# A fused attention and feed-forward kernel: keys' transposes moved from TensorE to VectorE and DRAM, first keys first, packed keys ahead of packed queries

## The reference

```python
x = L0_attn_x                                  # (16, 1024, 256)
xn = _layernorm(x, axis=-1)
x = x + attn(xn, Wqkv, Wout) + ffn(xn, W1, b1, W2, b2)

# attn: 16 heads of 16, segments of 512 rows; a segment's keys are every 8th row of it (64 keys)
scores = einsum('bhspd,bhskd->bhspk', q4, k4)             # q scaled by 16 ** -0.5
c = max(scores, over each block of 64 query rows)         # per key column
w = exp(scores - c)
out = einsum('bhsnmk,bhskd->bhsnmd', w, v4) / (sum(w, -1) + 1e-10)
return out @ Wout.T
# ffn
return relu(xn @ W1 + b1) @ W2 + b2                       # hidden width 1024
```

## Time and profile before

| | us |
|---|---|
| median of 3 runs | 1060.14 |
| lowest and highest | 1059.68, 1060.82 |
| the profiled execution, its device time | 1064.19 |
| its span from first to last instruction | 1062.2 |
| granted TensorE clock | 1.0 of full speed all through |

### The profile page before, as it was taken

How to read it: one execution, slowest core, us unless ns; L and a number is a source line. 1 busy time by engine, 2 the same in 40 slices (tenths; PEclk the granted TensorE clock), 3 DMA queues, 4 the chain that set the end, 5 groups by cost and what they waited for, 6 DMA issues and landing times.

```text
span 1062.2 us, 19202 instructions
## 1 busy us (share of the span) xinstructions
PE 1042.0 (98%) x5397; PEld 809.4 (76%) x5397; DVE 837.7 (79%) x1464; ACT 648.1 (61%) x1081; POOL 623.2 (59%) x489
## 2 busy tenths in 40 slices
PE   5999999999999999999999999999999999999998
PEld 4677777777787777787777777777877777877777
DVE  7987888878877887888878888788888878887752
ACT  5656665666666566666666656666565665656663
POOL 6355665656556556555656656565665565556564
PEclk9999999999999999999999999999999999999999
DMA  5157877687877778777778776868777787767754
GB/s 193 35 151 217 222 212 210 180 230 205 240 211 200 207 204 230 219 216 204 205 216 226 221 199 183 236 197 244 211 196 206 204 231 212 212 176 217 196 145 148
DMA packets 151895, 214.14 MB, mean 202 GB/s; under 512 B 27072, under 2 KB 95808, under 8 KB 151872
## 3 DMA queue, kind: packets, MB, share of 16 engines
q1 hardware_dynamic: 151728, 213.73, 72.4%
q10 hardware_dynamic: 144, 0.13, 0.0%
HBM read 100.01 MB, written 58.20 MB: 149 GB/s over the span
## 4 chain that ended last, share of the span: by engine, by line
PE 87%; DVE 5%; DMA 4%; issue 2%; SPq 1%; ACT 1%; DVEq 0%; ACTq 0%
PE h_bank L1081 38%; PE y_bank L1081 37%; PE s_banks L1156 5%; PE misc L1260 3%; PE s_banks L1260 2%; PE misc L1081 2%; DVE xn L858 1%; DMA k_pack<-k_dram 1%; DVE s_max L875 1%; DMA w_exp<-w 1%; DMA xt_dram<-z 1%; DVE w_exp L881 1%; DMA xt_raw<-xt_dram 1%; SPq L371 1%; DVE q_lo L924 0%
## 5 line engine op out<-in xcount | busy, mean ns | idle before, releaser
L534 POOL TENSOR_TENSOR h_lo<-h_full,h_hi 128x512 fp32r<-128x512 f32 x256 | 337.6, 1320 | 378.9 <-ACT h_full L625 376.9
L631 ACT ACTIVATE w_exp<-w_exp 128x512 f32<-128x512 f32 x256 | 161.6, 633 | 247.8 <-DVE w_exp L881 245.9
L623 ACT ACTIVATE h_hi<-h_bank,b_cols 128x512 fp32r<-128x512 f32 x256 | 174.7, 682 | 68.2 <-PE h_bank L1081 61.7
L1081 PE MATMUL h_bank<-xt_hi,w_hi 128*128 128x512 f32 x512 | 206.6, 403 | 0.0
L1081 PE MATMUL h_bank<-xt_lo,w_hi 128*128 128x512 f32 x512 | 200.3, 391 | 0.0
L1081 PE MATMUL h_bank<-xt_hi,w_lo 128*128 128x512 f32 x512 | 199.6, 390 | 0.0
L1081 PE MATMUL y_bank<-h_hi,w_hi 128*128 128x512 f32 x496 | 193.5, 390 | 0.2 <-ACT w_exp L631 0.2
L1081 PE MATMUL y_bank<-h_hi,w_lo 128*128 128x512 f32 x496 | 193.1, 389 | 0.0
L1081 PE MATMUL y_bank<-h_lo,w_hi 128*128 128x512 f32 x496 | 193.1, 389 | 0.0
L875 DVE TENSOR_REDUCE s_max<-s_banks 128x8 f32<-128x512 f32 x252 | 169.3, 672 | 29.0 <-PE s_banks L1156 28.5
L881 DVE TENSOR_TENSOR w_exp<-s_banks,s_max 128x512 f32<-128x512 f32 x252 | 174.2, 691 | 10.9
(11 more groups left out here) (146 smaller groups left out, 1542.6 us busy)
## 6 DMA issues: line engine op xcount, KB each, us to landing
q_pack<-q_hi SPq DMA_DIRECT2D x240, 128.0 KB, 2.5
rden_rows<-rden_dram SPq DMA_DIRECT2D x128, 128.0 KB, 4.6
x_b<-x SPq DMA_DIRECT2D x32, 512.0 KB, 4.7
x_raw<-x SPq DMA_DIRECT2D x31, 512.0 KB, 4.9
yt_dram<-y_mem SPq DMA_DIRECT2D x124, 128.0 KB, 3.5
y_mem<-yt_dram SPq DMA_DIRECT2D x31, 512.0 KB, 4.5
out<-x_b SPq DMA_DIRECT2D x31, 512.0 KB, 3.1
q_pack<-q_lo SPq DMA_DIRECT2D x120, 128.0 KB, 2.4
```

The costliest lines, as they stand in the source:

```text
L534: pool.tensor_tensor(h_part[1][:, i % HBUF], h_full[:, i % HBUF], f32(h_part[0][:, i % HBUF]), ALU.subtract).then_inc(h_lo, 1)
L623: act.activation(h_part[0][:, i % HBUF], h_bank[i % 2][:], ACT.Relu, bias=b1_cols[:, i:i + 1]).then_inc(h_hi, 1)
L631: act.activation(w_exp[:, pair], w_exp[:, pair], ACT.Exp).then_inc(w_ready, 1)
L1081: mm = pe.matmul(ps, stationary[a], moving[b], start=start and c == 0 and n == 0, stop=stop and c == len(pairs) - 1 and n == 2, skip_group ...
```

## The change

1. **Keys' blocks.** From step 2 on, PE no longer transposes the keys. At the end of an odd step, between the residual add and the transposes of y, DVE normalises the keys of the next even step and transposes their 32x32 blocks into a part of `z` (`transpose_key_blocks`). SP writes them to `xk_dram` in four DMAs (`key_blocks_to_dram`, after `pack(s, 1)`) and reads them back turned, into `xn_keys` (`keys_in`, after `den_spread`). ACT's `keys_hi` waits for that read, and `keys_hi` and `keys_lo` read SBUF in place of PSUM. For this POOL's `inverse_deviation` stands ahead of the tail's two `hidden_lo` in place of behind them. The large `transpose_blocks` of the even step, which writes the same `z`, waits for the keys' writes.
2. **Packed keys** are issued ahead of `pack(s, 0)`, and wait for all scores of the step, which read the old ones. The read of y is split in two halves, and where a step packs keys, the second half waits for the keys' writes to DRAM.
3. **The first step.** The first keys have statistics and `rstd` of their own ahead of the rows' ones. x of segment 1 is loaded behind two weights, and its statistics are taken later. ACT copies the first queries ahead of a half of w2. POOL clears `q_pack` in the lead step in place of the start. (Keys of segments 0 and 1, and of step 0, are still transposed by PE.)
4. **One residual add**, that of step 1, stands behind POOL's tile 4 in place of tile 2.

```diff
@@ SP
-                load_x(1, 1)
                 sp.dma_start(wkv_raw, ...)
                 sp.dma_start(wq_raw, ...)
+                load_x(1, 1)
...
             def pack_keys(s):
-                sp.wait_ge(k_out, (s + 1) * 32)
+                sp.wait_ge(s_psum, (s + 2) * PAIRS)
...
+            def key_blocks_to_dram(s):
+                sp.wait_ge(z_keys_ready, s + 1)
+                for i in range(P // PW):
+                    sp.dma_start(xk_dram[:, :, i].rearrange("j c n -> c j n"),
+                                 z_keys[PW * i:PW * (i + 1)]).then_inc(xk_out, 16)
+            def keys_in(s):
+                sp.wait_ge(xk_out, (s + 1) * 32)
+                sp.dma_start(xn_keys[:].rearrange("p (a k) -> p a k", a=DH),
+                             xk_dram.rearrange("(a j) c i n -> (j c) a (i n)", a=DH)).then_inc(xk_in, 16)
...
-            def y_from_dram(s):
+            def y_from_dram(s, keys):
                 sp.wait_ge(y_out, (s + 1) * 64)
-                sp.dma_start(y_mem[:, 1], ...).then_inc(y_in, 16)
+                for half, blocks in enumerate((slice(0, 2), slice(2, 4))):
+                    if half == 1 and keys:
+                        sp.wait_ge(k_out, (s + 2) * 32)
+                    sp.dma_start(y_back[:, blocks]..., yt_dram[:, :, blocks]...).then_inc(y_in, 16)
...
                 if norm:
+                    pack_keys(s)
                     pack(s, 0)
-                    pack_keys(s)
                     pack(s, 1)
+                if load and par == 1:
+                    key_blocks_to_dram(s)
                 if attention:
                     den_to_dram(s + 1)
                 if norm:
                     pack(s, 2)
                 if attention:
                     den_spread(s + 1)
+                if load and par == 1:
+                    keys_in(s)
@@ POOL
-                    if i == 2 and ffn:
+                    if i == (4 if isinstance(s, int) and s == 1 else 2) and ffn:
                         residual(s - 1, 1 - par)
...
+                if load:
+                    inverse_deviation(s + 3, 1 - par)
                 segment, tail = tail_tiles(s, attention)
                 for i in tail:
                     hidden_lo(segment, i)
-                if load:
-                    inverse_deviation(s + 3, 1 - par)
@@ ACT
             def keys_hi(s):
-                act.wait_ge(xkey_psum, s + 4)
+                if by_tensor(s):                      # s <= 0
+                    act.wait_ge(xkey_psum, s + 4)
+                else:
+                    act.wait_ge(xk_in, s * 8)
...
-                weight_hi(w2_half(w2_raw, 0), ...)
                 queries_hi(-2, 0)
+                weight_hi(w2_half(w2_raw, 0), ...)
@@ DVE, step
-                    if n == 0 and keys:
-                        normalise_keys(s + 2)
...
                 elif ffn:
+                    if load and par == 1:
+                        normalise_keys(s + 3)
+                        transpose_key_blocks(s + 3)
                     output_blocks(s)
@@ PE, step
-                    if i == KEY_TILES[0] and norm and par == 0:
-                        transpose_keys(s)
```

More of the change, by code:

```diff
@@ L246, in score_bank, with keys_transposed @@
             return s_bank[n % 2]
+        def keys_transposed(s):
+            return key_banks(s)[0][:, 0:DH * P] if by_tensor(s) else xn_keys[:]
         def transpose_banks(s):
@@ L277, in iterations, with tiles @@
                 fixed(s)
-        def tiles(par):
-            return T + 1 - par
+        def tiles(s, par):
+            return T if isinstance(s, int) and s == 0 else T + 1 - par
         def tile_steps(s, ffn):
@@ L447, in opening_step @@
                 keys_to_dram(0)
+                sp.wait_ge(k_out, 32)
+                pack_keys(0)
                 pack(0, 0)
-                pack_keys(0)
                 pack(0, 1)
@@ L583, in step, with first_keys_deviation @@
                     hidden_lo(segment, i)
-                if load:
-                    inverse_deviation(s + 3, 1 - par)
+            def first_keys_deviation():
+                pool.wait_ge(first_keys_stats, 1)
+                pool.wait_ge(consts_made, 3)
+                pool.tensor_tensor(var_eps[:, T:T + 1], mean_var[:, T:T + 1, 1], eps[:, T:T + 1],
+                                   ALU.add).then_inc(first_keys_var, 1)
+                pool.wait_ge(first_keys_var, 1)
+                pool.tensor_tensor(rstd[:, T:T + 1], var_eps[:, T:T + 1], minus_half[:, T:T + 1],
+                                   ALU.pow).then_inc(first_keys_rstd, 1)
+                pool.wait_ge(first_keys_rstd, 1)
             def first_step():
+                first_keys_deviation()
                 inverse_deviation(0, 0)
@@ L811, in mean_variance @@
             def mean_variance(s, par):
-                for t in range(tiles(par)):
+                for t in range(tiles(s, par)):
                     op = dve.bn_aggr(mean_var[:, t], stats_of(s)[:, t])
@@ L823, in normalise_keys, with keys_normalised @@
                 dve.wait_ge(rstd_ready, s + 1)
-                dve.wait_ge(xkey_psum, past(s))
+                if isinstance(s, int) and s <= 2:
+                    dve.wait_ge(xkey_psum, s)
+                else:
+                    dve.wait_ge(xkey_hi, s)
+                    dve.wait_ge(xkey_lo, s)
+                keys_normalised()
+            def keys_normalised():
                 dve.tensor_scalar(xn_keys[:], x_keys[:], mean_var[:, T, 0:1], rstd[:, T:T + 1],
@@ L862, in normalise, with transpose_key_blocks, transpose_blocks @@
                 op.then_inc(xn_ready, 1)
-            def transpose_blocks(s):
+            def transpose_key_blocks(s):
+                dve.wait_ge(xn_keys_ready, s + 2)
+                dve.transpose(z_keys, xn_keys[:].rearrange("p (j n) -> p j n", n=PW)).then_inc(z_keys_ready, 2)
+            def transpose_blocks(s, keys):
+                if keys:
+                    dve.wait_ge(xk_out, s * 32)
                 dve.wait_ge(xn_ready, s + 3)
@@ L1042, in first_step @@
                 drain_kv(-2)
+                statistics(1, 1)
                 statistics_done(1)
```

41 lines of the change are left out of this document (27 added, 14 removed).

## The result

| | before | after |
|---|---|---|
| median, us | 1060.68 (6 runs) | 1068.35 (6 runs) |
| lowest and highest | 1059.68, 1061.94 | 1065.67, 1069.67 |
| ratio, with its 95% interval | | 1.0069 (1.0057 to 1.008) |
| span of the profiled execution | 1062.2 | 1063.8 |

The kernel became 0.7% slower; the forecast was 1061.7 in a range of 1052 to 1073. The profile of after is of the fastest of its six executions, so a second one was taken later (1071.44, span 1069.6; the median of that series is 1067.32 beside 1061.37 for before, ratio 1.0049, 1.0031 to 1.0067). The second profile is of the slowest execution of its series. Both are read here. A stand is a stretch in which PE does nothing.

The account below looks back on a forecast made before the run. PE, busy 98% of the span, was taken as the bound. Terms -3.1 + 5.9 - 1.5 + 3.0 - 1.0 - 1.1 - 0.6 = +1.6 gave 1061.7 from 1060.14; own range 1056 to 1068, all cases 1052 to 1073.

Parts of the forecast that it names:

- Taken off PE: Two key transposes between products of y and h go, 0.22 in each of 14 even steps: -3.1 us.
- The keys' chain: Keys through DVE and DRAM reach PE's keys' projection late, 0.4 a step: +5.9 us (0 to +11).
- rstd is there at 485.1: Step 14, POOL: moved var_eps and rstd follow the statistics, taking 0.27 and 1.18.
- Late reads of y: Where y lands late, the keys behind the residual add come later too: +3 us (0 to 7.4).
- Packed keys first: PE's stands of 2.4 for packed keys go with their earlier issue: -1.5 us (0 to -2.4).
- Step 28: A third to two thirds of PE's 1.40 stand are left, as DVE is 1.3 ahead: -1.0 us.
- Step 1: Later residual add shortens DVE's xn; PE's 0.66 before queries and 0.3 before a score go: -1.1 us.
- The front: First step: ACT's copy of the queries ahead of w2 frees DVE before the first scores: -0.6 us (0 to -0.7).
- Rival (a): Keys arrive in time at the projection; +5.9 and most of +3 go: about 1054, chance 0.25.
- Rival (b): POOL's h_lo locks out DVE's denominators' guard; transpose_k stands 0.9 each even step: +12.6, about 1074, chance 0.12.
- Rival (c): Y's second half comes 0.5 behind DVE's need in every odd step: +7, about 1069, chance 0.13.

Follow-up runs that it names:

- experiment 10: Changed kernel with DVE normalising the keys and transposing their blocks ahead of the residual add, not behind it: 1072.77, ratio 1.0105 to before.
- experiment 11: Kernel of experiment 10 with the keys' read also issued ahead of the denominators' reads in SP's queue: 1071.98, ratio 1.0097 to before.
- experiment 7: Changed kernel with POOL's first tail h_lo waiting for the keys' normalisation, but packed queries first and y in one read again: 1058.05, ratio 0.9962 to before.
- experiment 8: Kernel before with only packed keys first and y read in halves: 1061.2 beside 1061.37, ratio 0.9994.
- experiment 2: Changed kernel without packed keys first, halves of y and later residual add; keys' new way and front stay: 1070.82, ratio 1.0093 to before.
- Experiment 1: Changed kernel with the keys' new way undone and inverse_deviation back behind POOL's tail, all else kept: 1059.2 beside 1060.63, ratio 0.9991.
- experiment 3: Changed kernel with the keys' read issued ahead of the denominators' two reads in SP's queue: 1059.68, ratio 0.9993 to before.
- experiment 5: Changed kernel with the keys' read issued later, behind the fourth packed queries in SP's queue: 1115.02, one execution.

## Why the prediction was right, and where it was off

The range held and the time came out on the slower side, as the sum had it, but with +7.3 and +5.2 us in the two series (by the ratios) in place of +1.6. The two medians lie at the edge of the forecast's own range (1056 to 1068); the rest of 1052 to 1073 is there for the rivals. By its own terms:

- **Taken off PE, -3.1:** right. The rows at 490.55 to 491.01 show it.
- **The keys' chain, +5.9:** the mechanism was right link by link (locked keys 1.22 to 1.39, issue 6.45 behind the blocks, read 2.27 to 2.47 where 2.4 was taken), its size was not. The stand is 0.4 to 1.2, 0.77 on average, where the sum had 0.3. Counted back from PE's need and averaged over the 14 steps of the first profile, the keys are normalised 0.25 later than forecast, the blocks take 0.55 in place of 0.45, issue and landing give back 0.04 each, and from the landing to PE's start are 1.20 in place of 1.0 (0.15 to ACT's start, 0.41, 0.1, 0.43, 0.1). The largest piece is the 0.25, and the step of the prediction that failed there is "rstd is there at 485.1", with nothing beside POOL: `rstd` took 1.18 from its old place, where no residual add runs beside it. At its new place it ends 0.3 to 0.9 later in 8 steps, which experiments 10 and 11 show by taking the add away, and in the other six the add stretches the h_lo that the keys wait for. The second piece, the 0.20 behind the landing, is starts and hand-overs that were priced at 0.2 and took 0.35. The bounds of 0 to +11 came from the read's price alone; the chain's 10.8, and 1.1 more with the slow first products, is at their upper end.
- **Late reads of y, +3:** right in place: 0 in the first profile and 4.4 in the second. In the first profile the three widest stands (1.05, 1.16, 1.20) have no late y ahead of them; they are the three in which the add meets `var_eps` as well as `rstd`.
- **Packed keys first, -1.5:** wrong. I took the waits of the earlier trace rows as gone and did not ask which transfer is late next in the same step. Experiments 7 and 8 put it at nothing (-0.6 us, interval -2.1 to +0.8).
- **Step 28, -1.0:** it lost 1.56 before, and 0.90 and 1.07 after. Right in sign, half the size.
- **Step 1, -1.1:** not shown. The forecast put PE's 0.66 before the queries down to POOL's residual add, which held DVE's `xn` (4.51). In the profiles of experiments 2 and 8 that add still stands at tile 2 and `xn` is as long, and PE doesn't stand there:

```profile
70.50 4.51 DVE L863 TENSOR_SCALAR xn<-x_raw,mean_var,rstd 128x256 f32<-128x256 f32 x4
```

This is experiment 8. What differs is the way of the queries' blocks: SP issues their read 2.2 behind the end of its four writes (78.14 to 80.33), and in the profile of before 3.6 behind (78.66 to 82.30). So the long `xn` alone costs PE nothing there; in the profile of before a late landing came on top of it.
- **The front, -0.6:** the first scores began at 18.11 and 17.49 in the two profiles in place of 18.67. The moved memset was in the diff and I priced it nowhere: in most profiles it costs PE nothing, in two a stand of 2.0 and a slow stretch of the clock.
- Experiment 1 has packs, step 1 and front together at -1.0, with an interval of -2.7 to +0.7; how that splits, only the profiles tell.

At the keys' projection the sum had 5.9 + 3 - 1.0 = 7.9. Of this 1.1 are the slow first products, which the table of losses leaves out: 6.8 to lay beside it. The two profiles have 10.8 and 14.1 less the 1.6 of before, 10.9 on average. That is 4.1 of the 4.7 that the sum missed on average; the packs are 0.9 to 1.5, and step 1 up to 1.1. Together that is more than 4.7 by less than the two series are apart (2.1).

**Rival (a)**, keys in time, did not come, but its price was near: with the lock taken away the kernel is at 1056.44 beside 1060.63, 4 faster than before, where (a) had 6 (1054). **Rival (b)** did not come either, but not for the reason given. The guard was forecast to be first by 0.1 or 0.2; in all even steps of the loop it starts 0.00 to 0.01 behind the h_lo and still runs in 0.18. For the forecast that was luck: 0.07 to 0.24 behind (experiment 3) it took 1.1 to 1.3. Such a guard came in step 28 of three profiles and in most steps of experiment 3. **Rival (c)**: the waits for y doubled, but PE doesn't lose by most of them.

One remedy was not tried. PE's first two products of the keys' projection read only `xkey_hi`, which is there 0.64 before PE starts; `xkey_lo` is read by the third. With the wait for it in front of that product, up to 0.5 of each stand would go by my estimate, from the 0.31 and 0.23 between the first three products.

## What to carry to other kernels

When an operation is moved on a queue, list what the other engine of a shared port does beside the new place, in both directions: who is locked out, and whom it locks out. In a chain with little slack the cheap places to win are the order in which a transfer is issued and which of two engines waits: one added wait turned 0.7% slower into 0.35% faster, and with the read issued sooner as well it was 0.66% faster. A wait that is taken away for one transfer is worth something only if the next transfer of the same step is not late too.

## What the runs showed of the hardware that was not expected

- When PE had been idle for up to 1.83 us the granted clock stayed at 1.00 (1.83 at 964.42 of experiment 10). Behind all 16 stands of 2.0 to 3.4 (14 in experiment 5, one each at the front of experiments 1 and 10) it was 0.50 to 0.70 in the next 3 us, and so it was behind one of 1.84, at 957.84 of experiment 11. The last column but two is the clock there. Two stands of nearly one length so ended differently. A stand of 2.5 behind which the clock falls costs 4.

```profile
957.84:960.84 3.00, 3.00 (x9) 2.38 (x10) 2.90 (x6) 1.75 (x3) 0.00 (x0) 0.65 0.92 202
```

- POOL's memset, which reads nothing, locks DVE's COPY out (2.30 for the first of two that together take 0.46) and not a TENSOR_TENSOR with two SBUF inputs that runs inside it (k_lo at 30.57, 0.42). The same page and section of the Trainium skill has both as rules, a copy in a two-port mode and the second input's read; the rows agree.
- The order of the recorded starts doesn't tell who gets the lock when they are close: `xn_keys` began 0.05 ahead of an h_lo and was locked out (492.46 and 492.51), while the guard began with or 0.01 behind one and was not. The two are different forms of operation; which of that decides was not tried. Of one form, `xn_keys` at 0.05 to 0.06 ahead took 1.50, and an `xn` 0.09 ahead (step 14 of before, 493.32 and 493.41) took its 0.40.
